# A transformer block on eight cores: later sums of exponentials on GpSimd, earlier 1/sqrt, and a later wq load in the first phase

## What is computed

```
h = layer_norm(x, ln1_g, ln1_b)
q = softmax((h @ wq) * scale, axis=-1)      # over the 256 of a head
k = softmax((h @ wk) * scale, axis=-2)      # over the 4096 rows
v = h @ wv
context = k^T v ;  attn = q context ;  x = x + attn @ wo + bo
...
```

## Time and profile before

| | |
|---|---|
| three runs | 1382.44, 1382.55, 1386.41 us; median 1382.55 |
| the profiled execution | 1383.19 us; spans of the cores 1378.5 to 1381.6 us |
| mean granted clock of TensorE | 0.998 to 0.999 on all cores |
| TensorE busy, slowest core (core 6) | 1353.3 us, 98% of its span |
| GpSimd's sums, L440 | 31, mean 2150 ns |
| ScalarE's exponentials, L431 | 28, mean 1027 ns |

### The profile page before, as it was taken

How to read it: one execution, slowest core, us unless ns; L and a number is a source line. 1 busy time by engine, 2 the same in 40 slices (tenths; PEclk the granted TensorE clock), 3 DMA queues, 4 the chain that set the end, 5 groups by cost and what they waited for, 6 DMA issues and landing times.

```text
span 1381.6 us, 17723 instructions; the slowest of 8 cores (1378.5 to 1381.6 us)
## 1 busy us (share of the span) xinstructions
PE 1353.3 (98%) x6484; PEld 626.9 (45%) x6484; DVE 557.7 (40%) x1020; ACT 390.3 (28%) x720; POOL 190.4 (14%) x103
## 2 busy tenths in 40 slices
PE   5999999999999999999999999999999999999997
PEld 4444444454444444444444444444444444444443
DVE  5765675256812111211123555632222222223566
ACT  4632333113763221122113445321111111111225
POOL 1522211217182000000100222200000000000000
PEclk9999999999999999999999999999999999999999
DMA  9844443298747830312101455460030100100113
GB/s 200 208 97 102 93 99 61 45 185 226 136 81 135 155 61 1 61 23 39 51 11 39 103 111 153 99 198 1 0 122 0 62 1 0 62 1 0 61 62 122
DMA packets 104773, 112.95 MB, mean 82 GB/s; under 512 B 90480, under 2 KB 90736, under 8 KB 102000
## 3 DMA queue, kind: packets, MB, share of 16 engines
q1 hardware_dynamic: 101664, 77.68, 22.0%
q0 software_dynamic: 2736, 33.56, 13.0%
q10 hardware_dynamic: 288, 0.59, 0.1%
HBM read 108.66 MB, written 8.39 MB: 85 GB/s over the span
## 4 chain that ended last, share of the span: by engine, by line
PE 93%; DMA 2%; DVE 2%; ACT 2%; issue 1%; DVEq 0%; ACTq 0%; SPq 0%; POOLq 0%
PE P L926 28%; PE P L1113 22%; PE P L897 16%; PE P L413 9%; PE P L471 5%; PE P L835 4%; PE P L1022 4%; PE P L696 2%; PE P L1079 2%; DMA xsA<-xkv 2%; DVE XHa L297 1%; DMA S<-wk 1%; ACT HT L391 1%; PE P L752 0%; PE P L727 0%
## 5 line engine op out<-in xcount | busy, mean ns | idle before, releaser
L926 PE MATMUL P<-S,GB 128*128 128x512 bf16 x1776 | 389.5, 379 | 0.0
L1113 PE MATMUL P<-T,S 128*128 128x512 bf16 x1408 | 305.7, 379 | 0.0
L933 DVE TENSOR_TENSOR R<-R,P 128x1024 f32<-128x1024 f32 x111 | 135.4, 1220 | 386.3 <-PE P L926 386.3
L926 PEld LDWEIGHTS P<-S,GB 128*128 128x128 bf16 x1776 | 173.7, 98 | 209.6
L897 PE MATMUL P<-T,S 128*128 128x512 bf16 x1024 | 225.1, 379 | 0.2 <-ACT GB L909 0.2
L1113 PEld LDWEIGHTS P<-T,S 128*128 128x128 bf16 x1408 | 137.8, 98 | 166.1
L413 PE MATMUL P<-S,HT 128*128 128x512 bf16 x704 | 156.8, 379 | 3.0 <-DVE HT L326 1.7
L897 PEld LDWEIGHTS P<-T,S 128*128 128x128 bf16 x1024 | 100.2, 98 | 121.2 <-issue 0.7
L909 ACT ACTIVATE GB<-P,pv 128x512 bf16<-128x512 f32 x128 | 86.0, 685 | 242.2 <-PE P L897 242.2
L1123 ACT ACTIVATE sl<-P 128x512 bf16<-128x512 f32 x88 | 52.4, 596 | 361.1 <-PE P L1113 355.1
L1126 DVE SCALAR_TENSOR_TENSOR GB<-sl,P 128x512 bf16<-128x512 bf16 x88 | 60.4, 687 | 208.5 <-PE P L1113 206.4
(11 more groups left out here) (114 smaller groups left out, 862.5 us busy)
## 6 DMA issues: line engine op xcount, KB each, us to landing
S<-wff POOLq DMA_DIRECT2D x8, 2048.0 KB, 17.3
xsA<-xkv SPq DMA_DIRECT2D x16, 512.0 KB, 6.3
xsB<-xkv SPq DMA_DIRECT2D x16, 512.0 KB, 4.2
R<-xkv SPq DMA_DIRECT2D x16, 512.0 KB, 10.4
xsD<-xkv SPq DMA_DIRECT2D x16, 512.0 KB, 4.1
y<-R SPq DMA_DIRECT2D x14, 512.0 KB, 2.7
S<-wgT SPq DMA_DIRECT2D x2, 2048.0 KB, 15.0
S<-wuT SPq DMA_DIRECT2D x2, 2048.0 KB, 14.9
```

Of the source, the lines that this page charges most:

```text
L926: tk = p.pe(lambda e, hc=hc, hf=hf: e.matmul(P[pr][:, hf * 512:(hf + 1) * 512], gb[:, hc * 512 + tile * 128:hc * 512 + tile * 128 + 128], ...
L933: t_R[i] = p.ve(lambda e: e.tensor_tensor(rrow(i), rrow(i), P[pr][:, :], ALU.add), tk, t_R[i])
L1113: tk = p.pe(lambda e, c=c, hc=hc, b=b, sw=sw: e.matmul(bank(b), S[sw][:, c * 1024 + hc * 128:c * 1024 + hc * 128 + 128], T[:, c * 2048 + t ...
```

## The change

- `K` no longer calls `acc_add`. A new function `sums(upto)` appends the sums of all tiles below `upto` that have not been put yet. The loop calls it from tile 11 on, `sums(min(2 * (i - 10), i + 1))`, and the last four tiles call `sums(i + 1)`. The calls of the first four tiles are gone.
- In steps 8 to 10 one A2 and A1 stand ahead of K(i), and the other pair behind the G block, where both stood before.
- K(11), K(13) and K(15) use bank pair 3 in place of 0.
- VectorE also takes the second half of the evictions of tile 8's transposes.
- wq's load stands behind step 10's second A2 and waits for `t_xt[14]`, the transposing transfer of tile 14; before, it stood ahead of K(6) and waited for the load of x tile 14.

```diff
--- before.py
+++ after.py
@@ -387,7 +387,7 @@
                 c = 4 * hb + k
                 src = pb[:, k * 128:(k + 1) * 128]
                 dst = ht[:, c * 512 + t4 * 128:c * 512 + t4 * 128 + 128]
-                if hb == 0 or j >= 8:
+                if hb == 0 or j >= 9:
                     t = p.se(lambda e, src=src, dst=dst, c=c: e.activation(
                         dst, src, AF.Identity, bias=pcol(B1, c), scale=pcol(G1, c)),
                         tk, t_pv, t_htfree[u % 2])
@@ -431,7 +431,14 @@
         t_E[i] = p.se(lambda e: e.activation(er(i), P[pr][:, :], AF.Exp, scale=0.25),
                       tk, g2, t_accs[i - 16] if i >= 16 else None)
         free[2 * pr] = free[2 * pr + 1] = t_E[i]
-        acc_add(i)
+
+    n_acc = [0]
+
+    def sums(upto):
+
+        while n_acc[0] < upto:
+            acc_add(n_acc[0])
+            n_acc[0] += 1
 
     def acc_add(i):
         if i == 0:
@@ -607,9 +613,17 @@
             A2(i + 1)
         if i < 11:
             T_tile(i + 1, i + 2 if i < 9 else None)
-        if i == 6:
-            t_wq = load_w("gpsimd", 1, wq_d, 0, t_x[14])
-        K(i, i % 2 if i < 8 else 0)
+
+
+        if 8 <= i < 11:
+            A2(2 * i - 6)
+            A1(2 * i - 5)
+        if i < 8:
+            K(i, i % 2)
+        else:
+            K(i, 3 if 11 <= i < 16 and i % 2 == 1 else 0)
+        if i >= 11:
+            sums(min(2 * (i - 10), i + 1))
         if 9 <= i < 12:
             G_add(0, i - 9, 1 + (i - 1) % 2)
         if own:
@@ -632,11 +646,11 @@
         if last and g >= 1:
             for f in range(4):
                 unit(u + 1, f)
-
         if 8 <= i < 11:
-            for j in (2 * i - 6, 2 * i - 5):
-                A2(j)
-                A1(j + 1)
+            A2(2 * i - 5)
+            A1(2 * i - 4)
+        if i == 10:
+            t_wq = load_w("gpsimd", 1, wq_d, 0, t_xt[14])
         if i >= 11:
             A(i)
         if i >= 11:
@@ -644,6 +658,7 @@
 
     for i in range(28, 32):
         K(i, 0 if i % 2 == 0 else 1)
+        sums(i + 1)
         G_pass(2, i - 24, 3 - i % 2)
         G_add(2, i - 24, 3 - i % 2)
     t_kdone = t_htfree[1]
```

## The result

The changed kernel takes 1396.25 us, the median of 16 runs, against 1386.59 for 16 runs of the kernel before taken in the same way. The ratio of the undisturbed runs is 1.0086, 95% interval 1.0066 to 1.0106: **slower by about 0.9%**. The prediction said slower by 0.4%, 1388.5 us, range 1379 to 1394; the time lies above the range. Disturbed runs, in which the cores of one die were slowed, are left out of every ratio here, and of e2's profile, where cores 0 to 3 were slowed so, cores 4 to 7 alone are read.

The account below looks back on a forecast made before the run. TensorE, busy 1353.3 of 1381.6 us, was taken as the bound, with 6.11 us of waits in reach. 1383.19 plus 4.1 (held L326, net of savings) plus 1.8 (clock) gave 1389.1; against the median 1388.5 us, range 1379 to 1394.

Parts of the forecast that it names:

- Steps 1 and 2: Catch-up tiles: no sums before tile 11 wins 2.73 us of L297 waits; earlier statistics and pair 3 win 1.54 at K(11).
- step 2: K(11): statistics ahead of the exponentials and pair 3 remove its wait for K(10)'s exponential to free pair 0, 1.54 us won.
- Step 3: wq behind tile 14's transfer, issued until about 69.1, shares DMA engines with tile 15's transfer, landing at 72.6 to 75.0 us.
- Step 4: GpSimd: nothing paces the sums; copy and eleven sums run back to back from 69.1 until about 96 us.
- Step 5: scale_x(3): one sum before each of eight L326, seven more periods, 15.8 us; K(12) ends at 92.4, net +4.1 us.
- rivals A and B: L326 series: A, it passes after one hold, 1376.4 us, chance 0.18; B, two L326 for each sum, 1379.1, chance 0.10.
- Step 6: TensorE's clock falls in the stall before K(12) ends; the first 3.6 us after run at half pace, +1.8 us.
- Rival C: Tile 15: copy catches A2(15), transfer slow beside wq, clock low twice as long, two more periods; 1394.8 us, chance 0.10.

Follow-up runs that it names:

- e2: Changed kernel with each sum from tile 11 on also waiting for that step's exponential, two a step; ratio 1.0034 to the kernel before.
- e6: Kernel before with only the sums deferred to tile 11 and paced two a step; ratio 0.9993 to the kernel before.
- e5: Kernel before with only the change's order, pair 3 and tile 8's evictions on VectorE, sums and wq as before; ratio 0.9961 to the kernel before.
- e4: Kernel before with wq alone moved behind tile 14's transposing transfer; ratio 1.0057 to the kernel before.
- e10: Changed kernel with wq alone moved back behind the load of x tile 14, sums unpaced; ratio 0.9985 to the kernel before.
- e7: Changed kernel with wq loaded in sixteen pieces behind tile 14's transfer, sums unpaced; ratio 1.0048 to the kernel before.
- e11: Changed kernel with wq in sixteen pieces behind tile 14's transfer and the sums paced two a step; ratio 0.9996 to the kernel before.
- e3: Changed kernel with wq behind tile 15's transfer and the sums paced two a step from tile 11; ratio 0.9967 to the kernel before.
- e1: Changed kernel with wq waiting for tile 15's transposing transfer instead of tile 14's, sums unpaced; ratio 1.0038 to the kernel before.

## Why the prediction was wrong

**Steps 1 and 2 held.** T(11) was forecast for 64.54 and came at 64.09, K(11) for 71.89 and came at 71.44; both are early by what T(5) was early. The waits for L297 went with the deferred sums (e6). The wait for L431 at K(11) goes with the order alone (e5) and also with the deferred sums alone (e6), which the reading in step 2 does not account for. At K(12) the order alone wins all of the 1.84 us, as it brings tile 15's transfer ahead of the sum that held the L326 (e5); the deferred sums alone leave 0.9 us of waiting (e6).

**Step 3 failed: the transfer beside wq.** GpSimd issued wq at 68.46, forecast 68.4. But "shares the DMA engines with tile 15's transfer ... lands at 72.6 to 75.0" was wrong: it landed at 86.5. The bound was taken from landings beside loads of x (4.7 to 5.4 us), half a megabyte each in packets of 4 KB; no row of the kernel before had a transposing transfer beside wq's 2 MB in packets of 16 KB for its whole length. e4 and e10 show that wq's place makes the loss, e2 that the sums have no part in the late transfer, e7 and e11 that wq in pieces of about 1 KB a packet does not hold it (5.7 and 6.1 us). That the size of the packets is the reason is the likeliest reading, not shown: in e7 and e11 most of wq was also issued later than the transfer. The Trainium skill (DMA: Bandwidth & Descriptors, "Queues, rings and completion order") says that each DMA engine goes round between the queues it has work for, a whole packet at a time. The trace agrees from 76 to 84 us, with 72 packets of the transfer beside 73 of wq's, and in e3 with 67 of an x load beside 71. It does not from 70 to 76 (8 beside 55), nor in e7 (984 beside 143), so the profile's packets are not always passed one for one. By that rule, as an estimate, the transfer's 66 packets on an engine (1056 on 16) are mostly still to come when wq's eight big ones (128 on 16) are through, and it lands with the end of wq, which took 17.4 us in the kernel before. That would have given about 86, near the measured 86.5.

**Step 4 held**: copy and eleven sums in one piece, 68.98 to 94.93 (forecast 69.1 to about 96).

**Step 5 held in its mechanism**: one sum before each L326 at a period of 2.26 us, against rivals A and B, in the changed kernel and in e1. Its size did not: the late transfer met only the last four sums, so the eight took 9.8 us instead of 16.3.

**Step 6 was mis-sized.** The clock fell, as taken. K(12)'s last matmuls and the G block behind it should have ended by 97.5 + 3.45; they ended at 104.21, so the low clock cost 3.3 us, where 1.8 were forecast and 3.6 was the bound.

The terms: transfer 11.5 us later than taken, L326 6.5 shorter, clock 1.5 more; 6.5 of the 6.6 us between the forecast's 5.9 and the 12.5 of core 6. That the sign came out right is no proof of the sum: its largest error, 11.5 us, was more than half hidden by the opposite one in step 5. Rival C, 1394.8 us, came nearest and named a transfer slow beside wq, but got there by a longer series of held L326, and the series was shorter.

## What to carry to other kernels

Before a large load is moved, list the small transfers that will be in flight beside it and who waits for them: a bulk load that was harmless early holds a transfer of small packets where that is needed at once. Here the same bytes in pieces held it far less, but the best place for the load was the early one. Work that is called at a step is not done at that step: an operation queued without a wait of its own runs as soon as its engine is free, so a deferred backlog comes in one piece unless each part waits for something of the step. Where an engine's short operations and another's long ones exclude each other, each short one may cost a long one (2.26 us for each L326 here), which is why the backlog must be kept clear of a series of them.

## What was not expected of the hardware

- A transposing transfer that lands in 3.0 us alone took 15.2 to 17.6 us beside a 2 MB load in 16 KB packets (all cores of the changed kernel, core 6 of e2 and e4), and 5.7 and 6.1 beside the same bytes in pieces with packets of about 1 KB (e7, e11).
- Such a transfer can also block the queue that issues it: in e3 the issue itself took 10.35 us on SP, and a load of x behind it was late by that.
- Between VectorE and GpSimd, which exclude each other here, the sum that started 0.07 to 0.08 us after an L326 went first each time: the three such pairs of the changed kernel's core 6 and the five of e1's.
- TensorE's clock did not come back with the first matmuls behind the stall: it read 0.50 from 84 to 96 and 0.57 from 96 to 102, and cost 3.3 us.
